# One attention loop over 64 units, batch outside and head inside, with the output projection gathered in PSUM inside the loop

## The reference

```
xn = layernorm(x)
q  = rope(xn @ Wq.T)                       # 16 heads of D = 128
kp, vp = split(xn @ Wkv.T)                 # one shared key and value, 128 wide each
kh, vh = cumulated, gated factors          # one number a token and head
k = rope(kp * kh),  v = vp * vh            # per head
p = softmax(causal(q @ k.T / sqrt(D)))
x = x + layernorm((p @ v, heads side by side) @ Wout.T)
x = x + layernorm(moe(layernorm(x)) + shared_mlp(layernorm(x)))
```

## Time and profile before

| what | us |
|---|---|
| median of 3 runs | 920.63 |
| lowest, highest | 919.33, 924.89 |
| span of the profiled execution | 903.7 |

### The profile page before, as it was taken

How to read it: one execution, slowest core, us unless ns; L and a number is a source line. 1 busy time by engine, 2 the same in 40 slices (tenths; PEclk the granted TensorE clock), 3 DMA queues, 4 the chain that set the end, 5 groups by cost and what they waited for, 6 DMA issues and landing times.

```text
span 903.7 us, 16151 instructions
## 1 busy us (share of the span) xinstructions
PE 804.7 (89%) x4566; PEld 641.4 (71%) x4566; DVE 682.2 (75%) x1671; ACT 542.6 (60%) x1340; POOL 455.6 (50%) x438
## 2 busy tenths in 40 slices
PE   4789999989898899999989898979879999999993
PEld 3666667667666699667667666768867788887772
DVE  6769998999999643899899999875667356665476
ACT  2557677767777654677677777766745235543242
POOL 2255555555555554455555555537727543331783
PEclk9989999999999899999999999999999999999996
DMA  9121102110111000101110211111032134431332
GB/s 346 43 97 58 41 25 52 46 46 23 58 46 44 26 0 0 48 18 52 46 46 23 58 46 33 31 48 48 1 125 88 70 134 173 169 132 59 95 89 96
DMA packets 30191, 60.52 MB, mean 67 GB/s; under 512 B 3792, under 2 KB 14416, under 8 KB 29648
## 3 DMA queue, kind: packets, MB, share of 16 engines
q1 hardware_dynamic: 26656, 51.10, 17.1%
q0 software_dynamic: 3072, 8.39, 2.9%
q10 hardware_dynamic: 432, 0.66, 0.3%
HBM read 43.09 MB, written 17.04 MB: 67 GB/s over the span
## 4 chain that ended last, share of the span: by engine, by line
PE 57%; DVE 14%; ACT 12%; issue 10%; POOL 5%; DMA 1%; ACTq 1%; DVEq 0%; POOLq 0%
PE ps L749 12%; PE ps L800 12%; PE ps L317 11%; PE ps L815 8%; PE ps L786 5%; ACT split_hi L525 4%; PE ps L896 3%; POOL work L1594 3%; DVE split_lo L1124 3%; ACT x_sb L496 3%; DVE wq_hi L1065 1%; DVE neg_max L1113 1%; PE ps L753 1%; PE ps L967 1%; PE ps L962 1%
## 5 line engine op out<-in xcount | busy, mean ns | idle before, releaser
L1493 POOL TENSOR_TENSOR work<-work,rope_sb 128x512 f32<-128x512 f32 x64 | 82.0, 1281 | 221.4 <-ACT work L489 221.4
L496 ACT ACTIVATE x_sb<-ps,neg_max 128x512 f32<-128x512 f32 (+3 forms) x256 | 134.1, 548 | 95.3 <-DVE neg_max L1113 95.2
L749 PE MATMUL ps<-work 128*128 128x512 f32 (+3 forms) x512 | 164.2, 443 | 2.5 <-POOL work L1500 1.6
L1139 DVE TENSOR_SCALAR x_sb<-x_sb,row_inv 128x512 f32<-128x512 f32 (+3 forms) x256 | 131.1, 533 | 6.8
L1113 DVE TENSOR_REDUCE neg_max<-ps 128x1 f32<-128x512 f32 (+3 forms) x256 | 112.0, 483 | 31.2 <-PE ps L753 31.2
L525 ACT ACTIVATE split_hi<-ps,vcol 128x512 fp32r<-128x512 f32 (+3 forms) x256 | 114.0, 530 | 27.0 <-PE ps L786 27.0
L800 PE MATMUL ps<-split_hi,w_hi 128*128 128x512 f32 (+3 forms) x256 | 89.9, 351 | 39.9 <-DVE split_lo L1124 39.9
L1124 DVE SCALAR_TENSOR_TENSOR split_lo<-ps,vcol,split_hi 128x512 fp32r<-128x512 f32 (+3 forms) x256 | 122.9, 537 | 2.0 <-ACT split_hi L525 2.0
L749 PEld LDWEIGHTS ps<-work 128*128 128x128 f32 x512 | 83.1, 191 | 43.0 <-issue 23.7
L800 PEld LDWEIGHTS ps<-split_hi,w_hi 128*128 128x128 f32 x256 | 48.8, 191 | 76.4 <-issue 63.8
L1537 POOL TENSOR_TENSOR split_lo<-arena,split_hi 128x256 fp32r<-128x256 f32 x88 | 66.6, 777 | 49.5 <-ACT split_hi L546 49.5
(11 more groups left out here) (200 smaller groups left out, 1920.1 us busy)
## 6 DMA issues: line engine op xcount, KB each, us to landing
work<-kvh_rows SPq DMA_DIRECT2D x64, 256.0 KB, 3.3
slot_inputs<-arena SPq DMA_DIRECT2D x4, 1280.0 KB, 11.9
arena<-slot_inputs SPq DMA_DIRECT2D x8, 640.0 KB, 4.6
slot_outputs<-arena SPq DMA_DIRECT2D x8, 640.0 KB, 3.3
x_sb<-in_x_dram SPq DMA_DIRECT2D x8, 512.0 KB, 5.5
arena<-in_w_up_dram SPq DMA_DIRECT2D x8, 368.0 KB, 4.8
wo_raw<-in_wout_dram SPq DMA_DIRECT2D x16, 128.0 KB, 2.0
arena<-in_w_dn_dram SPq DMA_DIRECT2D x8, 256.0 KB, 3.8
```

Source lines behind the costliest of these rows:

```text
L496: ins = act.activation(prob[:, r, ROW_AT[nt]:ROW_AT[nt] + w], ps_s[bank][:, at:at + w], ACT.Exp, bias=neg_max[:, r, nt:nt + 1], accum_out= ...
L749: pe.matmul(ps_s[bank][:, at:at + w], q_rot[:, r, nt * P:(nt + 1) * P], k_h[:, r, 0:w], start=(nt == tiles[0]), stop=False)
L1139: ins = dve.tensor_scalar(p_, p_, row_inv[:, r, nt:nt + 1], None, ALU.mult)
L1493: pool.tensor_tensor(q_sw, q_sw, sin_sb, ALU.mult).then_inc(q_sin_ready, 1)
```

## The change

1. **Order.** One loop over 64 units, written out in full (no `Fori`), with the batch outside: unit i is head i % 16 of batch i // 16.
2. **Weights stay.** All of Wq and Wout is loaded at the start in four pieces each and lies split in SBUF; ACT makes the "hi" parts and POOL the "lo" parts, 4 heads (1,024 elements a partition) at a time. Two Wq pieces are split ahead of the loop, six pieces in steps 0 to 10. DVE splits none.
3. **Sums divide the output.** The probabilities are not divided. One reciprocal a unit (`inverses`) is stored as a row of DRAM (512 elements of 4 bytes, each with an address of its own), read back as a row broadcast to 128 partitions, and DVE multiplies the unit's output with it while it takes it from PSUM (`divide_output`).
4. **Projection in the loop.** ACT copies the output to `o_hi`, POOL makes `o_lo`, and PE adds the unit before to two PSUM banks that collect a batch over its 16 heads (`gather_output`, six matmuls of 512 columns).
5. **Banks.** Queries and unit outputs share bank 0. The third scores bank is also the third bank of turned probabilities. PE runs the scores two units ahead.
6. **Layer norms in the loop.** For batches 0 to 2, in steps 17 to 20, 33 to 36 and 49 to 52: ACT copies the collected banks, PE turns them back (8 transposes), DVE copies them, takes statistics, normalizes; POOL adds x; DVE takes statistics again. ACT's two square roots lie between exponentials. Batch 3 has the same work after the loop. x isn't read again.
7. **After attention.** The slot groups are (batches 0 to 2) and (batch 3). The clearing of the slots moves from the start of the kernel into steps 4 to 11.

The buffers are placed by hand in one slab; those moves follow from the above.

```diff
+        def head(i):
+            return i % H
+        def batch(i):
+            return i // H
+        def back_step(b):
+            return H * (b + 1) + 1
+        WQ_STEP = {WCH * c - 5: c for c in range(2, WC)}
+        WO_STEP = {max(0, WCH * c - 2): c for c in range(WC)}
...
+            def spread_inverse(i):
+                sp.wait_ge(inv_ready, i + 1)
+                with nc.allow_non_contiguous_dma(reason="a column of sums becomes a row"):
+                    sp.dma_start(inv_dram[i:i + 1, :].rearrange("a (t p) -> p (a t)", p=P), row_inv[:, i % 2, :]) \
+                        .then_inc(inv_stored[i % 2], 16)
+                sp.wait_ge(inv_stored[i % 2], 16 * (i // 2 + 1))
+                if i >= 2:
+                    sp.wait_ge(o_ready, i - 1)
+                sp.dma_start(inv_row[:, i % 2, :], inv_dram[i:i + 1, :].to_broadcast([P, SEQ])) \
+                    .then_inc(inv_row_in[i % 2], 16)
...
+            for i in range(UNITS):
+                if i + 5 < UNITS:
+                    load_kh_row(i + 5)
...
+                if i + 2 < UNITS:
+                    spread_inverse(i + 2)
```

ACT's loop:

```diff
+            for i in range(UNITS):
+                for b in range(B - 1):
+                    if i == back_step(b):
+                        copy_gathered(b)
+                heads_of_turned(i)
+                if i + 3 < UNITS:
+                    swap_q(i + 3)
+                if i == UNITS - 1:
+                    turned_head(0)
+                    x_normed(1)
+                if i + 2 < UNITS:
+                    exps(i + 2)
+                if i == UNITS - 2:
+                    x_normed(0)
+                head_of_output(i)
...
+                for b in range(B - 1):
+                    if i == back_step(b):
+                        deviations(b, 0)
+                    if i == back_step(b) + 2:
+                        deviations(b, 1)
```

PE's:

```diff
-            def steps(h, last):
-                for b in range(B):
...
-                    pe.wait_ge(prob_ready, i + 1)
...
+            def gather_output(i):
+                h, b, r = head(i), batch(i), i % 2
...
+                pe.wait_ge(o_lo_ready, i + 1)
+                for eh in range(EO):
+                    es = slice(eh * P, (eh + 1) * P)
+                    for j, (w, o_) in enumerate(((wo_hi, o_hi), (wo_lo, o_hi), (wo_hi, o_lo))):
+                        ins = pe.matmul(ps_acc[eh][:], w[:, h, es], o_[:, r, :],
+                                        start=(h == 0 and j == 0), stop=(h == H - 1 and j == 2))
+                ins.then_inc(proj_psum, 1)
...
+            for i in range(UNITS):
+                turn_probs(i)
+                if i + 3 < UNITS:
+                    queries(i + 3)
+                for b in range(B - 1):
+                    if i == back_step(b):
+                        turn_back(b)
+                if i + 2 < UNITS:
+                    scores(i + 2)
+                if i == UNITS - 1:
+                    turn(0)
+                weigh_values(i)
+                if i:
+                    gather_output(i - 1)
+            turn(1)
+            gather_output(UNITS - 1)
+            turn(2)
```

`weigh_values(i)` waits for the swap and the cosine of the queries of unit i + 3 and for `divide_output(i - 1)`, since they share the bank. `turn_probs(i)` waits for the exponentials of unit i + 1 ahead of its third bank. DVE's and POOL's:

```diff
-                for nt in tiles:
-                    w = P * (nt + 1)
-                    p_ = prob[:, r, ROW_AT[nt]:ROW_AT[nt] + w]
-                    ins = dve.tensor_scalar(p_, p_, row_inv[:, r, nt:nt + 1], None, ALU.mult)
...
+            def divide_output(i):
+                dve.wait_ge(o_psum, i + 1)
+                dve.wait_ge(inv_row_in[i % 2], 16 * (i // 2 + 1))
+                if i:
+                    dve.wait_ge(o_lo_ready, i)
+                dve.tensor_tensor(o_t[:], ps_qo[:], inv_row[:, i % 2, :], ALU.mult).then_inc(o_ready, 1)
...
+            for i in range(UNITS):
+                rest_of_turned_probs(i)
+                if i + 3 < UNITS:
+                    cos_q(i + 3)
+                for b in range(B - 1):
+                    if i == back_step(b):
+                        take_back(b)
+                if i + 2 < UNITS:
+                    maxima(i + 2)
+                for b in range(B - 1):
+                    if i == back_step(b):
+                        stats_of_y(b)
+                    if i == back_step(b) + 1:
+                        normalize_y(b)
+                    if i == back_step(b) + 2:
+                        stats_of_x2(b)
+                    if i == back_step(b) + 3:
+                        scale_x2(b)
...
+                divide_output(i)
+                if i + 2 < UNITS:
+                    inverses(i + 2)
...
+            for i in range(UNITS):
+                if i:
+                    rest_of_output(i - 1)
+                if i + 3 < UNITS:
+                    scale_keys(i + 3)
...
+                if i + 3 < UNITS:
+                    sin_q(i + 3)
+                    rotate(i + 3)
```

After the loop DVE does batch 3's norms and then `choose(0)` for twelve token tiles. PE's order there:

```diff
+            logits(0)
+            turn_back(B - 1)
+            shared_up(0, [0])
...
+            shared_up(0, range(2, SH))
+            shared_up(1, [0])
             positions(0)
+            shared_up(1, range(1, SH))
```

More of the change, by code:

```diff
@@ new lines, in decoder_layer, with small @@
+        SW0 = ROPE + 4 * KB
+        small_at = [SW0 + EO * 2 * SHID * 4]
+        def small(name, shape, dt=F32):
+            size = int(np.prod(shape)) * (2 if dt == BF16 else 4)
+            at = small_at[0]
+            small_at[0] += -(-size // 32) * 32
+            assert small_at[0] <= SLAB
+            return place(name, at, shape, dt)
+        x_sb = place("x_sb", X_AT, [TILES, E])
+        xt_hi = place("xt_hi", XT_HI, [EO, T], F32R)
+        xt_lo = place("xt_lo", XT_LO, [EO, T], F32R)
@@ L539, in head_of_outputs @@
-            def head_of_outputs(g, t):
-                for c in range(OC):
-                    if c < OC - 1:
-                        act.wait_ge(oc_used, (g * TILES + t) * (OC - 1) + (c + 1))
-                    elif not (isinstance(t, int) and g * TILES + t == 0):
-                        act.wait_ge(proj_psum, g * TILES + t)
-                    act.copy(oc_hi[:, c, :, :], o_t[:, 2 * c:2 * c + 2, bass.ds(t * P, P)]).then_inc(oc_hi_ready, 1)
-            with act.Fori(0, HG) as h:
-                steps(h, h, False)
@@ new lines, in heads_of_turned @@
+            def heads_of_turned(i):
+                for k, tiles in enumerate(PT_BANKS):
+                    act.wait_ge(pt_psum, 3 * i + (k + 1))
+                    if i:
+                        act.wait_ge(o_psum, i)
+                    for mt in tiles:
+                        bank, at = pt_slot(mt)
+                        w = SEQ - mt * P
+                        col = batch(i) * H + head(i)
+                        ins = act.activation(pt_hi[:, COL_AT[mt]:COL_AT[mt] + w], ps_pt[bank][:, at:at + w],
+                                             ACT.Copy, scale=vcol[:, mt, col:col + 1])
+                    ins.then_inc(pt_hi_ready, 1)
@@ L868, in _ @@
-            pe.wait_ge(o_free, UNITS + 1)
-            for t in range(TILES):
-                project(1, t, ps[5 + t % 2 * 2])
-                if t % TPB == 2 and t >= 2 * TPB:
-                    turn(t // TPB - 2)
-            logits(0)
+            pe.wait_ge(consts_made, 1)
+            pe.wait_ge(k_cos_ready, B)
+            queries(0)
+            pe.wait_ge(hc_ready, 1)
+            for mt in range(TPB):
+                ins = pe.transpose(ps[3][:, mt * P:(mt + 1) * P], hc_t[:, mt * P:(mt + 1) * P], id_f[:])
@@ L1328, in _, with shared_hidden @@
-            scale_and_shift(B - 2, 1)
-            y_stats(B - 1)
-            choose(0)
-            scale_and_shift(B - 1, 0)
-            find_slots(0)
-            def shared_hidden(j):
-                for i in range(SH):
+            def shared_hidden(j, tiles=range(SH)):
+                for i in tiles:
                     w = SHW[i]
```

1058 lines of the change are left out of this document (486 added, 572 removed).

## The result

| | kernel before | changed kernel |
|---|---|---|
| median, four runs each | 919.98 us | 1137.13 us |
| lowest, highest | 916.41, 924.89 | 1129.57, 1139.09 |
| ratio, 95% interval | | 1.2344 (1.2275 to 1.2414) |

The changed kernel is 217 us slower, where 38.7 less was forecast.

What follows compares the result with a forecast made beforehand. PE was taken to bound the kernel at 8.25 us a unit. Head 2, shared-weight split 1, loop 544.5 and tail 84.8 gave 632.3 against 671.0, 38.7 less: 882 us against 920.6, range 868 to 898.

Steps and rivals of the forecast that it cites:

- The trip of the inverses: Loop, store and reload of inverses through DRAM: store lands in 2.0 to 5.0 us, taken as 4; row's latency hidden.
- SP's line of stores decides: Rival, loop: from 7.2 us a store each unit waits for its row; at 9 us, 986 us in all; chance 0.09.
- PE's unit, 8.25: Loop: PE's pieces for a unit sum to 6.86 us, plus 1.39 for six new matmuls, 8.25 a unit.
- The tightest hand-over: Loop, bank shared by queries and outputs: values may write it with 0.3 us to spare.
- I take that 1.3% on the whole loop: Loop: the layout fell 1.3% short of the old kernel's head, so 537.5 us was raised to 544.5.
- Norms, 19.5: Loop, layer norms of batches 0 to 2: 6.5 us a batch on the chain, 19.5 for three, bounds 0 and 45.
- The norms land in full: Rival, layer norms in the loop: 45 us in place of 19.5, 907 us in all; chance 0.10.
- The table switch costs the page's price: Rival, ACT's roots in the loop: twelve switches at 2.66 us each add some 8 us, 890 in all; chance 0.05.
- The weights, 2, and the head, +2: Weight pieces in steps to 10 add 2 us (bounds 0 and 15); start before the loop adds 2 (bounds -2 and +5).
- The loop, 544.5, and the tail, 84.8: Loop to unit 63's transposes takes 544.5 us; from there to the first expert's transposes 84.8.
- PE full and nothing late: Rival, whole rebuilt part: no 1.3% and norms half hidden, 865 us; chance 0.06.
- The 16.9 us around it: Whole kernel: 16.9 us outside the profiled span, added to the span of 865 to give 882.

Runs made afterwards that it cites:

- the kernel without the trip: Changed kernel with SP neither storing nor loading the inverses, the dividing row holding ones: 855.18 us beside 907.38 of the kernel before, ratio 0.9412.
- the kernel that divides the probabilities: Changed kernel with DVE dividing the probabilities again and no trip of the inverses: 862.85 us beside 907.38, ratio 0.9516; on another chip 883.18 beside 918.35.

## Why the prediction was wrong, point by point

- **The step that failed: "The trip of the inverses".** The term was the store, "2.0 (that size is free) to 5.0 us", "I take 4". It measured 11.5, so the condition "under 8.25 as long as the store takes under 7.2" broke and SP's line set the unit. The lower bound came from a store of long runs. The upper one added the packets' time, 32 x 93 ns, and took it for all that small pieces cost. That time was even too dear: 93 ns is a mean over packets of mostly 2 KB, and one of 4 bytes takes 9 ns. What the sum has no term for is the time behind the packets, 6.6 us in this store. Nor is the number of packets the cause (the run with the pieces 64 bytes apart has as many and takes 1.9); their place in DRAM counts. Why neighbouring pieces land late stays open.
- **"What isn't free is SP."** Right, and so was the rival *SP's line of stores decides*, in its mechanism: SP's period is the store plus about 1.0. It was worked out for stores of 8 and 9 us (986 for the latter). With 11.5 in it the period is 12.5 a unit, measured 12.63, and from 8.35 up that gives 63 x 4.15 = 261 us; the loop lost 260.1 to the trip. It had 0.09. Against it stood only that "it needs over twice the time that the packets' mean gives": an argument from the same unfit row, used twice. What the rival left out is that the store also holds up what runs beside it, so that even without SP's line 167 us of the loop stayed.
- **The Trainium skill on this form** (DMA: Bandwidth & Descriptors, Rules for kernel authors): one descriptor per element. The packets agree: 128, 256 and 512 pieces a store give 46,880, 55,072 and 71,456 packets on SP's queue, 64 x 128 and 64 x 256 apart. Their cost doesn't follow from the number.
- **PE's unit, 8.25.** Measured 8.27 or 8.28 in every plain unit of the kernel without the trip, from step 2 on and transposes to transposes:

```profile
150.98 1.25 PE L789 MATMUL ps<-id_f,prob 128*128 128x128 f32 x10
159.26 1.25 PE L789 MATMUL ps<-id_f,prob 128*128 128x128 f32 x10
167.54 1.25 PE L789 MATMUL ps<-id_f,prob 128*128 128x128 f32 x10
```

- **"The tightest hand-over", 0.3 us.** Holds: PE waits in the whole loop for DVE's "lo" parts 8.9 us, for the shared bank not at all.
- **"I take that 1.3% on the whole loop."** Not there: 8.28 is 0.4% over the layout. The old loop's shortfall wasn't one that a kernel carries over.
- **Norms, 19.5.** Measured 0.88 + 1.87 + 1.24 = 4.0 a batch over the plain unit, in the first, second and fourth of the four steps, 12 for three: oversized, and the rival *The norms land in full* falls. The table loads took their bare 1.28, with the root right behind and nothing idle ahead:

```profile
219.57 1.28 ACT L564 ACT_TABLE_LOAD   x1
220.86 0.30 ACT L564 ACTIVATE std<-mv,eps_sb 128x4 f32<-128x4 f32 x1
...
223.44 0.58 ACT L523 COPY q_sw<-ps 64x512 f32<-64x512 f32 x1
224.04 1.28 ACT L533 ACT_TABLE_LOAD   x1
```

  The drain of about the same length that the Trainium skill adds (ScalarE: Activation LUTs, What ACT_TABLE_LOAD costs) isn't in these rows, and *The table switch costs the page's price* falls with it. Its price was mis-sized too: twelve times the prediction's own 2.66 less 1.28 us is 16.6, where it says some 8 without a working.
- **The weights, 2, and the head, +2.** Step 1 took 9.58, 1.3 over the plain unit, and no other step to 10 was longer; the changed kernel's first transposes came at 64.2 after 62.55. Right to within 1 us, both of them; without the trip the first transposes came at 67.0, and why isn't known.
- **The loop, 544.5, and the tail, 84.8.** 535.3 and 80.9 without the trip, 13.1 us less; the span was 855.6 for the forecast's 865. The ratio 0.9412 on the 920.6 of the prediction is 866.5: for all but the trip *PE full and nothing late*, at 865, was the right case, and 882 two per cent too high.
- **"The 16.9 us around it."** Wrong. A profiled run's own time is its span plus 1.9 (915.0 and 916.93 for the kernel before). By these signs the 16.9 lay between two chips: the profile has none of the waits in the tail, its 903.7 being a run of about 905.6, and the times are those of a chip with them. (Which chip the first profile came from isn't on record.) From one chip to the other the kernel before gains 11 us (907.38 to 918.35), the kernel that divides the probabilities 20 (862.85 to 883.18), so a ratio moves by about 0.01 with the chip and the verdicts don't.
- **The clock "isn't a rival".** It fell to 0.90 in the loop, but as a result: PE idled first (308 to 310 us above). The chain through the stores doesn't pass through it.

## What to carry to other kernels

A DMA that writes pieces of 4 bytes side by side in DRAM can hold up every other DMA: before it goes into a loop, look for a form that gives each partition's pieces a run of 16 bytes or a place of their own (both were fast here), and let the engine that reads the row put up with the order. Where no row of the trace has the form of a new transfer, the nearest row is no bound; ask at which latency the plan breaks (here 7.2 us), and measure that transfer first. When the chain names a DMA, look at the landing times of the transfers beside it as well: if they grow too, the transfer doesn't only take long, it holds up the others. And compare two spans only when the chip is the same or the difference is placed by stage: 19 of the 279 us here were no part of the change.

## What the runs showed of the hardware

- A store of 512 pieces of 4 bytes lands after 11.5 us when they lie side by side (sixteen from as many partitions in 64 bytes), 4.2 when they are 8 bytes apart, 1.9 when they are 64 bytes apart; 128 pieces of 16 bytes take 1.4.
- The packets of these stores take about 9 ns each in every form. What differs is the time from the last packet to the landing: 6.6 us side by side, 0.6 with 64 bytes between them, 0.4 for 16-byte pieces.
- While such a store is out, loads of 256 KB take 9.9 us in place of 3.1, on the same queue and (10.7) on another, though in the changed kernel the DMA engines' share reads 0.00 for half of the time to landing.
- Chips differ in the tail: on two of three, engines beside the indirect scatters wait some 19 us or more for nothing that the trace names, with the kernel before as with the changed one.
- DVE reads every fourth element of a row, fp32, at 1.06 us for 512 where it takes 0.69 in order.
